# A Flamingo-like block, batches chained: the next batch's scan starts among the finished batch's attention products

## The reference, cut to what matters

```python
# batch 4, length 512, width 512; context width 256; 16 states; feed-forward 2048
x = x + tanh(g_xattn[0]) * mamba(ctx, layernorm(x))          # conv, dt, scan over 512 steps, gate
x = x + tanh(g_ffn[0])   * bitlinear_ffn(layernorm(x))       # ternary weights, 8-bit rows
x = x + tanh(g_xattn[1]) * (layernorm(x) @ softmax(q @ k.T)) # q, k from ctx alone
x = x + tanh(g_ffn[1])   * (gelu(layernorm(x) @ p1.T + b1) @ p2.T + b2)

def mamba(ctx, z):
    x = silu(conv(ctx @ in_proj.T) + conv_b)                  # 512 channels
    dt_low, Bm, Cm = split(x @ x_proj.T)
    dt = softplus(dt_low @ dt_proj.T + dt_b)
    # per channel and state n: h[t] = h[t-1] * exp(dt[t] * A[n]) + dt[t] * x[t] * Bm[n, t]
    # y[t] = sum over n of h[t] * Cm[n, t]
    return (y + D * x) * silu(z)
```

## Time and profile before

| | us |
|---|---|
| median of 3 runs (lowest, highest) | 975.09 (974.25, 976.95) |
| profiled execution | 976.27 |
| its span, first to last instruction | 974.2 |
| TensorE busy | 824.5 (85%) |
| VectorE busy | 776.4 (80%) |
| ScalarE busy | 660.9 (68%) |
| GpSimd busy | 520.0 (53%) |

### The profile page before, as it was taken

One profiled execution on the slowest core, in us unless ns is written; L12 is line 12 of the kernel. 1 busy time (PEld: TensorE's weight loads), 2 busy tenths in 40 slices (PEclk: granted clock), 3 DMA queues, 4 the chain that ended last, 5 costly groups with the idle time before them and its releaser, 6 DMA issues. The chain is left out here.

```text
span 974.2 us, 9381 instructions
## 1 busy us (share of the span) xinstructions
PE 824.5 (85%) x2810; PEld 405.8 (42%) x2810; DVE 776.4 (80%) x905; ACT 660.9 (68%) x984; POOL 520.0 (53%) x461
## 2 busy tenths in 40 slices
PE   6721246799799999999799999998999998898999
PEld 2210012344344344454344444443443444456887
DVE  4589997895889998986899998977889997863333
ACT  4599979573699973774699863773799863624442
POOL 0598785211899883203999881215998871012000
PEclk9755558899899999999899999999899999999999
DMA  8079985001199967301499964301699972201231
GB/s 298 11 142 205 269 202 100 1 1 44 30 201 234 235 145 192 108 2 43 86 212 231 242 140 127 109 1 43 123 225 212 218 164 74 109 1 44 87 108 65
DMA packets 47969, 123.74 MB, mean 127 GB/s; under 512 B 5920, under 2 KB 7072, under 8 KB 47408
## 3 DMA queue, kind: packets, MB, share of 16 engines
q0 software_dynamic: 17280, 62.92, 34.3%
q1 hardware_dynamic: 30640, 60.24, 18.2%
HBM read 56.03 MB, written 4.19 MB: 62 GB/s over the span
## 5 line engine op out<-in xcount | busy, mean ns | idle before, releaser
L1668 POOL TENSOR_TENSOR work<-du,bcast 128x1024 f32<-128x1024 f32 x128 | 352.4, 2780 | 33.8 <-ACT bcast L867 33.2
L1271 DVE TENSOR_TENSOR_SCAN pair<-pair,work 128x512 f32<-128x512 f32 x256 | 299.3, 1215 | 34.4 <-ACT pair L882 28.9
L882 ACT ACTIVATE pair<-dt,a_neg 128x512 f32<-128x512 f32 x256 | 165.8, 682 | 20.2 <-DVE work L1278 17.2
L653 PE MATMUL bank<-stage,ring 128*128 128x512 f32 x384 | 172.9, 593 | 1.5 <-ACT stage L1116 1.5
L1278 DVE TENSOR_TENSOR work<-pair,ccast 128x1024 f32<-128x1024 f32 x128 | 156.8, 1225 | 11.6
L1679 POOL DMA_DIRECT2D u<-work x120 | 130.8, 1090 | 49.0 <-DVE work L1278 20.5
L438 PE MATMUL bank<-xd,pick 128*128 128x512 bf16 x128 | 56.3, 440 | 88.1 <-ACT bcast L867 61.8
L653 PEld LDWEIGHTS bank<-stage,ring 128*128 128x128 f32 x384 | 71.8, 190 | 80.5 <-issue 70.9
L1654 POOL TENSOR_SCALAR fst<-fst 128x1 f32<-128x1 f32 x32 | 9.2, 288 | 166.7 <-DVE fst L1505 166.5
L667 PE MATMUL bank<-ring,stage 128*128 128x512 f32 x192 | 85.6, 594 | 1.7 <-ACT hx L1151 1.7
L438 PEld LDWEIGHTS bank<-xd,pick 128*128 128x128 bf16 x128 | 13.1, 102 | 140.6 <-ACT bcast L867 90.1
(11 more groups left out here) (168 smaller groups left out, 1519.9 us busy)
## 6 DMA issues: line engine op xcount, KB each, us to landing
u<-work POOLq DMA_DIRECT2D x120, 512.0 KB, 6.0
ring<-ffn_dram SPq DMA_DIRECT2D x120, 256.0 KB, 5.0
ring<-ffn_dram SPq DMA_DIRECT2D x16, 512.0 KB, 3.3
xres<-x_dram SPq DMA_DIRECT2D x4, 1024.0 KB, 5.4
stage<-w_dram SPq DMA_DIRECT2D x1, 4096.0 KB, 16.9
stage<-w_dram SPq DMA_DIRECT2D x4, 1024.0 KB, 7.4
out_dram<-stage SPq DMA_DIRECT2D x16, 256.0 KB, 2.1
ctxT<-ctxT_dram SPq DMA_DIRECT2D x4, 512.0 KB, 6.8
```

The source lines that it names most:

```text
L653: last = pe.matmul(banks[2 + f % 2][:], piece(b, f)[:, k * P:(k + 1) * P], xnT[:, k, :], start=k == 0, stop=k == J - 1)
L882: act.activation(pairs[s % DECAYBUFS][:, q, :], dt[:, p * HALF + q, :], ACT.Exp, scale=a_neg[:, p * HALF + q, n:n + 1]).then_inc(s_decay, 1)
L1271: dve.tensor_tensor_scan(pair[:, q, :], pair[:, q, :], rows[:, q, :], 0.0, ALU.mult, ALU.add).then_inc(s_scan, 1)
L1668: pool.tensor_tensor(work[:, s % SCANBUFS, :, :], du[:, p * HALF:(p + 1) * HALF, :], bcast[:, n % 2, :].unsqueeze(1).broadcast_to([P, HALF ...
```

## The change

`attend` writes to banks 1 and 2 in turn and `norm_transpose` only to bank 3, so the scan's pairs no longer wait for `third`. Instead `attend` 2 and 3 wait for `third` 0 and 1, and the first query product for `third` 2. `third` 1, 2, 3 and `norm_apply` 4 to 7 move behind single halves of slots 4 and 5 on VectorE, with their transposes, copies and norms. The up products begin at place 2 of slot 5 instead of 0 and end at place 1 of slot 9; two down pairs more stand in the turning, behind the first three gate transposes. The product of the last but one state (n = 14) is added to `u` by a GpSimd instruction instead of a DMA, with a semaphore of its own, which `last_sum` waits for.

The diff, with the declaration of the semaphore and those hunks left out that only follow it (the copies' bank on ScalarE, and steps that leave an old place):

```diff
@@ -59
 W_LATE = (("scale", 1, 2), ("sign", 1, 2), ("scale", 1, 3), ("sign", 1, 3))
-ATT_BANKS = (4, 6, 7, 6)
+ATT_BANKS = (1, 2, 1, 2)
 MEAN_BANK = 2
...
-FFN_UP = {(5 + f // 4, f % 4): f for f in range(FT)}
-FFN_DOWN = {(9, 0): (0, 0), (9, 1): (0, 2), (9, 2): (0, 4), (10, 0): (0, 6), (10, 1): (0, 8), (10, 2): (0, 10), (10, 3): (0, 12), (11, 0): (0, 14), (11, 2): (1, 0), (11, 3): (1, 2), (12, 0): (1, 4), (12, 1): (1, 6), (12, 2): (1, 8), (12, 3): (1, 10)}
-FOURTH_SLOTS = {(11, 0): 0}
+FFN_UP = {(5 + (f + 2) // 4, (f + 2) % 4): f for f in range(FT)}
+FFN_DOWN = {(9, 2): (0, 0), (9, 3): (0, 2), (10, 0): (0, 4), (10, 1): (0, 6), (10, 2): (0, 8), (10, 3): (0, 10), (11, 0): (0, 12), (11, 1): (0, 14), (11, 2): (1, 0), (11, 3): (1, 2), (12, 0): (1, 4), (12, 1): (1, 6)}
+FOURTH_SLOTS = {(11, 1): 0}
...
@@ -488
             pe.wait_ge(s_qk, b * 2 + 1)
+        elif prev is not None:
+            pe.wait_ge(s_x3, prev * T + 3)
         for k in range(KC):
@@ -567
         gate_transposes(m, (2,))
+        f_pair(b, 1, 8)
+        f_pair(b, 1, 10)
         f_pair(b, 1, 12)
@@ -609
-        bank = 3 if i < T else 2 + i % 2
         if i < T:
             pe.wait_ge(s_x2, b * T + i + 1)
+            pe.wait_ge(s_ev1, b * T + min(i + 2, T))
         else:
             pe.wait_ge(s_xn, b * T + i - T + 1)
-        if i < T:
-            pe.wait_ge(s_ev1, b * T + min(i + 2, T))
-        if i == T - 1:
-            pe.wait_ge(s_xnTc, b * 2 * T + T - 1)
-        if i == T:
-            pe.wait_ge(s_ev0, b * T + T)
-        if i > T:
-            pe.wait_ge(s_xnTc, b * 2 * T + i - 1)
+        if i:
+            pe.wait_ge(s_xnTc, b * 2 * T + i)
         for k in range(J):
             rows = xb[:, i, :] if i < T else xn[:, i % 2, :]
-            last = pe.transpose(banks[bank][:, k * P:(k + 1) * P], rows[:, k * P:(k + 1) * P], ident[:])
+            last = pe.transpose(banks[3][:, k * P:(k + 1) * P], rows[:, k * P:(k + 1) * P], ident[:])
         last.then_inc(s_xnT, 1)
...
         pe.wait_ge(s_xnTc, b * 2 * T + t + 1)
-        if t == 1 and m is not None:
-            pe.wait_ge(s_dt, m * J + J)
         if t == 0:
-            pe.wait_ge(s_gelu, b * T * FC + T * FC)
             pe.wait_ge(s_att, b * J + J)
-        if t == T - 2:
-            pe.wait_ge(s_x2, b * T + T)
-        if t == T - 1:
-            pe.wait_ge(s_x3, b * T + 2)
+            if m is not None:
+                pe.wait_ge(s_dt, m * J + 2)
+        elif t == 1:
+            pe.wait_ge(s_ev0, b * T + T)
+        else:
+            pe.wait_ge(s_x3, b * T + t - 1)
         for k in range(J):
@@ -753
         down1(b, 3)
-        attend(b, 0)
         norm_transpose(b, 2)
-        attend(b, 1, m)
+        attend(b, 0, m)
         scan_bcast(m, 0, 0)
+        norm_transpose(b, 3)
+        attend(b, 1)
+        scan_bcast(m, 1, 0)
         attend(b, 2)
-        scan_bcast(m, 1, 0)
-        norm_transpose(b, 3)
-        norm_transpose(b, 4)
         scan_bcast(m, 0, 1)
         attend(b, 3)
-        norm_transpose(b, 5)
@@ -808
                 qk_products(m, prev, 0)
+            if rest and slot == 5:
+                norm_transpose(b, 5)
             if rest:
@@ -817
                 if rest:
-                    norm_transpose(b, 6)
-                    norm_transpose(b, 7)
+                    norm_transpose(b, 4)
+            if rest and slot == 5:
+                norm_transpose(b, 6)
             if rest:
...
             attention(m, slot, 1, 0)
+            if rest and slot == 5:
+                norm_transpose(b, 7)
             if rest:
@@ -888
                 act.wait_ge(s_dt, b * J + J)
-                if prev is not None:
-                    act.wait_ge(s_x3, prev * T + 1)
                 decay_half(b, 0)
             if n == 0 and part == 0 and prev is not None:
-                act.wait_ge(s_x3, prev * T + T)
+                act.wait_ge(s_x2, prev * T + T)
             if 2 * n + 1 + part < HN:
...
@@ -1174
                 weights(slot)
+            if rest and slot == 5:
+                norm_copy(b, 5)
             if slot != 4:
@@ -1182
                 if rest:
-                    norm_copy(b, 6)
-                    norm_copy(b, 7)
+                    norm_copy(b, 4)
+            if rest and slot == 5:
+                norm_copy(b, 6)
             if rest:
...
             attention(m, prev, slot, 1, 0)
+            if rest and slot == 5:
+                norm_copy(b, 7)
             decays(m, prev, slot, 1, 1)
@@ -1357
         step_inputs(m, 1)
-        norm_apply(b, 4)
-        third(b, 1)
-        norm_apply(b, 5)
-        third(b, 2)
-        third(b, 3)
@@ -1409
         dve.wait_ge(s_hc, (b * HN + HN - 1 + p) * HALF)
-        dve.wait_ge(s_acc[p], (b + 1) * (NS - 1) * 16)
+        dve.wait_ge(s_sum, b * HALF + p + 1)
         dve.tensor_tensor(u[:, js, :], u[:, js, :], work[:, (HN - HALF + p) % SCANBUFS, :, :],
@@ -1591
             if rest and slot == 4:
+                third(b, 1)
+                norm_apply(b, 4)
+            if rest and slot == 5:
+                third(b, 3)
                 norm_apply(b, 6)
+            half(m, prev, slot, 0, 1)
+            if rest and slot == 4:
+                third(b, 2)
+                norm_apply(b, 5)
+            if rest and slot == 5:
                 norm_apply(b, 7)
-            half(m, prev, slot, 0, 1)
             if rest and (slot, 0) in FOURTH_SLOTS:
...
             half(m, prev, slot, 1, 0)
+            if rest and (slot, 1) in FOURTH_SLOTS:
+                fourth(b, FOURTH_SLOTS[slot, 1])
             half(m, prev, slot, 1, 1)
@@ -1616
             state_input(b, prev, p)
-            if prev is not None:
-                norm(prev, T + 2 + p)
+            if prev is not None and p == 0:
+                norm(prev, T)
         for j in range(J):
...
                                ALU.mult, ALU.mult).then_inc(s_accin, 1)
+        if prev is not None:
+            norm(prev, T + 1)
         for s in range(2, AHEAD):
...
@@ -1664
             m, q = divmod(s - SCANBUFS, 2)
-            pool.wait_ge(s_acc[q], (b * (NS - 1) + m + 1) * 16)
+            pool.wait_ge(s_acc[q], (b * (NS - 2) + m + 1) * 16)
         pool.tensor_tensor(work[:, s % SCANBUFS, :, :], du[:, p * HALF:(p + 1) * HALF, :],
@@ -1674
         if n:
-            pool.wait_ge(s_acc[p], (b * (NS - 1) + n) * 16)
+            pool.wait_ge(s_acc[p], (b * (NS - 2) + n) * 16)
         carry_wait(pool, "pool")
-        pool.dma_start(u[:, p * HALF:(p + 1) * HALF, :], work[:, s % SCANBUFS, :, :],
-                       accum_op=ALU.add).then_inc(s_acc[p], 16)
+        js = slice(p * HALF, (p + 1) * HALF)
+        if n == NS - 2:
+            pool.tensor_tensor(u[:, js, :], u[:, js, :], work[:, s % SCANBUFS, :, :], ALU.add).then_inc(s_sum, 1)
+        else:
+            pool.dma_start(u[:, js, :], work[:, s % SCANBUFS, :, :], accum_op=ALU.add).then_inc(s_acc[p], 16)
@@ -1770
         for slot in range(4, SLOTS):
-            if rest and slot == 5:
-                bias(b, 2)
             half(m, prev, slot, 0, 0)
             if rest and slot == 4:
+                norm(b, 6)
+            if rest and slot == 5:
                 bias(b, 0)
-            if rest and slot == 5:
-                bias(b, 3)
+            if rest and slot == 6:
+                bias(b, 2)
             if not rest:
...
             if rest and slot == 4:
+                norm(b, 7)
+            if rest and slot == 5:
                 bias(b, 1)
+            if rest and slot == 6:
+                bias(b, 3)
             half(m, prev, slot, 1, 0)
...
```

More of the change, by code:

```diff
@@ L267, in program @@
         s_acc = [sem(f"s_acc{p}") for p in range(HALF)]
+        s_sum = sem("s_sum")
         s_last = sem("s_last")
@@ L1007, in between @@
                 first_copy(m, b, 0, 1)
-                norm_copy(b, 4)
             def closing(b):
@@ L1111, in norm_copy @@
                     act.wait_ge(s_xm, b * T + t + 1)
-                bank = 3 if i < T else 2 + i % 2
                 if parts:
                     act.activation(in_parts(x_high[:, :, t * P:(t + 1) * P]),
-                                   banks[bank][:].rearrange("p (k l) -> p k l", k=J), ACT.Copy)
-                act.activation(xnT[:, :, t * P:(t + 1) * P], banks[bank][:].rearrange("p (k l) -> p k l", k=J),
+                                   banks[3][:].rearrange("p (k l) -> p k l", k=J), ACT.Copy)
+                act.activation(xnT[:, :, t * P:(t + 1) * P], banks[3][:].rearrange("p (k l) -> p k l", k=J),
                                ACT.Copy).then_inc(s_xnTc, 1)
@@ L1167, in pass_ @@
                         decays(m, prev, slot, 0, 1)
-                        if rest:
-                            norm_copy(b, 5)
                     copy_next(m, slot, 0, 0)
@@ L1636, in between @@
                 norm(b, 3)
-                norm(b, 4)
-                norm(b, 5)
                 start_sum(m, b)
```

## The result

The changed kernel takes 1025.8 us (median of 4 runs, 1024.05 to 1026.5) against 975.05 (974.25 to 976.95) of the kernel before on the same chip: ratio 1.0506, 95% interval 1.0485 to 1.0527. The forecast was 998 us, 982 to 1007. The direction was right; the loss is 50.7 us where 22.6 were summed up. The profiled execution has a span of 1024.5 us (before 974.2).

What follows compares the result with a forecast made beforehand. TensorE, busy 197.75 of a pass's 212.1 us, was taken as the bound, VectorE second. Three passes x 8.1, first scan -2.1 and closing +0.4 gave +22.6 us, so 998 us, range 982 to 1007.

Steps and rivals of the forecast that it cites:

- Part 1: Start of the scan in a pass: it begins 3.4 us earlier, at 459.65.
- Part 2: Start of the up products: 8.8 us later, at 484.1, with 1.2 us taken for stalls of four applies.
- Part 6: Behind the gates: q's transpose moves 8.1 us later per pass, closing +0.4; DMAs, bias additions and moved norms cost nothing.
- Part 3: TensorE's clock at the start of the up products: half rate costs 1.5 us, bounds 0 and 2.6.
- Part 4: Up and down products: first up to first down stays 62.2 us; then two pairs save 6.87, fewer waits 2.2.
- Part 5: Last partial sum: its 3.2 us DMA wait goes, off the path in passes; the first scan gains 2.1 us.
- (c): Rival, worse: applies stall 4.7 us, clock costs 2.6, few waits won back; 1008 us; 0.15 including no earlier scan.
- (b): Rival, faster: work fills TensorE's 5.45 us hole, up products start no later than 475.27; 970 us; chance 0.07.

Runs made afterwards that it cites:

- e7: Changed kernel with norm_apply also writing out a sum nobody reads, a form that doesn't take the shared port: 1005.53 us, ratio 1.0306.
- e8: e6 with the four applies per pass on ScalarE, and the third half's decays and one GpSimd norm moved: 959.18 us, ratio 0.9825.
- e10: e8 with the change's feed-forward tables: up products two places later, matching down products, two pairs behind the gates: 978.92 us, ratio 1.0031.
- e6: Changed kernel rebuilt: thirds 1, 2 and applies 4, 5 ahead of the scan, feed-forward tables of before, bias additions late: 989.12 us, ratio 1.0137.
- e1: Kernel before with one part of the change alone, state 14's product added to u by GpSimd instead of a DMA: 973.55 us, ratio 0.9972.
- e11: e9 with ScalarE's applies 4 and 5 one place earlier and half 3's decays behind the next broadcast copies: median 968.59 us, ratio 0.9927.
- e2: Changed kernel with the four GpSimd bias additions two slots later, nothing else: 1012.69 us, ratio 1.0366.
- e9: e1 plus the four applies per pass on ScalarE, scan still behind all four attention products: 981.96 us, ratio 1.0063.
- e4: Changed kernel with 24 idle bf16 matmuls on TensorE ahead of the last norm transpose: 1023.06 us, ratio 1.0474.

## Why the prediction was wrong in size

**Part 1, the scan's start: right** within 0.2 us. **Part 2: the step that failed**, in its term for the stalls of the applies. "I take 0.3 (nearest to the median), 1.2 in all", bounds 0 to 2 each. Measured in the three passes: the fourth apply 6.40, 6.39 and 6.38, another one 2.06, 1.60 and 3.25. What the four take beyond 0.52 each is 7.4, 7.0 and 8.6 us a pass for the 1.2 taken: 19.4 us too little in three passes. Up to the start of the last apply the forecast held: it comes 37.1 us behind the end of `down1` (460.50 to 497.62), for 36.7 by its terms (445.04 to 481.7). From there to the first up product 2.4 us were forecast, and it took 8.25. e7, where no apply stalls, has the 38.6 that the terms give. Of the 27.6 us that the sum missed, this row of the table has 19.7. Of the sixteen applies in the earlier trace rows three met one product of GpSimd (2.57 each) and the others gaps or short instructions. The change sets the last one behind a product, with a bias addition, a DMA issue, a second product and a second bias addition ready behind it. GpSimd, kernel after:

```profile
495.44 2.64 POOL L1673 TENSOR_TENSOR work<-du,bcast 128x1024 f32<-128x1024 f32 x1
497.75 1.55 POOL L1739 TENSOR_TENSOR stage<-stage,b 128x512 f32<-128x512 f32 x1
498.96 1.18 POOL L1688 DMA_DIRECT2D u<-work  x1
499.56 2.95 POOL L1673 TENSOR_TENSOR work<-du,bcast 128x1024 f32<-128x1024 f32 x1
501.87 1.86 POOL L1739 TENSOR_TENSOR stage<-stage,b 128x512 f32<-128x512 f32 x1
508.93 0.90 POOL L1688 DMA_DIRECT2D u<-work  x1 [5.21 <-issue]
```

The apply, begun at 497.62, ends at 504.01, 0.3 us behind the end of this run of five instructions (503.73). A bound of 2 us, less than one product, was the mistake: here the apply waited until GpSimd's run ended. The third apply shows the same from the other side: it ends at 494.12, 0.3 behind the end of one product (493.83), after which GpSimd stood still for 0.09 us only. "Bias additions ... move on GpSimd, which has room: nothing" (Part 6) was wrong for the same reason: it has room, but their place closed the gap in which VectorE would have got in.

That GpSimd has no idle time isn't enough by itself. In the kernel before, the two applies at 466.65 took 0.78 and 0.91 while GpSimd's instructions stood back to back:

```profile
465.12 2.86 POOL L1623 TENSOR_SCALAR u<-u,pch 128x512 f32<-128x512 f32 x4
467.95 4.81 POOL L1668 TENSOR_TENSOR work<-du,bcast 128x1024 f32<-128x1024 f32 x2
```

In that run each record begins within 0.03 us of the end of the one before; in the runs that held VectorE for 5.65 to 6.40 each begins 0.3 to 0.6 us ahead of it (by spans that are rough). What decides whether VectorE is let in between two instructions stays open: no run varies it.

The Trainium skill (SBUF — State Buffer, "Who interferes with whom") says that whoever starts first holds the shared pair for its whole instruction, and that the form of `tensor_scalar` that also writes out its accumulator doesn't use it. The second agrees with e7 (0.77 to 0.81 us, always). By the first the wait would have been at most one product, 2.95 us; 6.39 says that VectorE wasn't let in between these instructions of GpSimd. The measurement decides.

**Part 3, the clock: right in kind.** Three stretches, ahead of the last wait, at the start of the up products and 5 us on (columns as in the earlier trace rows):

```profile
496.00:497.00 1.00, 0.61 (x1) 0.11 (x1) 0.90 (x2) 0.68 (x2) 1.00 (x1) 0.50 0.91 176
506.00:508.00 2.00, 2.00 (x3) 0.97 (x4) 1.91 (x3) 0.38 (x1) 0.00 (x0) 0.50 0.00 0
511.00:513.00 2.00, 2.00 (x6) 0.95 (x5) 2.00 (x3) 1.32 (x2) 2.00 (x3) 1.00 1.13 197
```

The clock is at 1.2 GHz already at 496, before the wait of 7.22 begins (496.86), and at 2.4 GHz again by 511. The stalled apply isn't its cause: in e7, whose longest wait there is 1.57, it is 0.50 as well (488.3 to 498.5). The first eight matmuls take 5.54 for 3.70: 1.8 us for the 1.5 taken. The Trainium skill (TensorE: Matmul & The Clock Gate, "Part 4: PE-mode transpose") says that transposes don't count as activity. No run shows transposes alone: among short transposes and broadcasts with waits under 1.7 us the clock fell in e7 and stayed at 1.00 in e8.

**Part 4, up to down: "62.2 us as before" was wrong by 3.9.** 1.8 is the clock, 1.2 the longer wait of the first down group for ScalarE, 0.9 two energy products that moved in from the next stretch. "Moving their places by one state keeps their order against the rest" isn't so: e10 has 3.5 of it without any stalled apply, 1.4 of them the clock again. **Down to gates:** -7.9, -8.1, -8.0 for -9.1. 6.9 are the two pairs and 0.9 the energy products that left this stretch, so in sum next to nothing was won back, for 2.2 taken. TensorE's idle time fell by 0.7 only (3.35 to 2.64), and the clock took some 2 us: the group of sixteen down products at 607.89, behind a wait of 2.10 for `fourth`, which the change puts one place later, takes 9.05 us where 7.03 is the full rate. A last -1.6 isn't split here.

**Part 5: right.** The last sums don't wait, the first gates come 3.0 earlier (2.1), the rest is off the path. **Part 6: right**, 6.8 per turning for 6.87; the closing gained 1.0 instead of losing 0.4.

**The rivals and the range.** (c) named the cause, stalls beside GpSimd, and still priced them at half a product each. Its sum is wrong as well: 8.1 and its own 3.5, 1.1 and 1.2 make 13.9 a pass and 1015, not 11.5 and 1008. The upper end of the range, 10.5 a pass, leaves out the forecast's own bound of 2 us for each apply: with it and the other upper bounds the terms make 17.2 a pass, 1025. That this is the measured time is luck, since a single apply went beyond its bound by far. (b) said what a faster version needs: up products before 30.2 behind the end of `down1`, and work in the hole. e8 is such a version (26.0), with the feed-forward tables of before. e6, the same idea with the applies on VectorE, lost 14 us.

So of the change's parts: GpSimd's addition gains 3 us (e1), the early scan is worth between 2 (e8 against e11's faster executions) and 9 (by the medians), the half slot costs about 20 (e10 against e8, the clock's part in it), and the stalled applies about 20 (e7 against the change), 13 of which are the bias additions' place (e2). These were measured in different surroundings and needn't add up.

## What to carry to other kernels

Before moving a VectorE instruction of a two-port form into a stretch where GpSimd is busy, list what GpSimd has ready behind it: in these runs the stall lasted up to the end of a whole run of GpSimd instructions, at the least to the end of one product, and a median from a stretch with other neighbours says nothing on it. If such an instruction stands on the path of the bounding engine, give it to ScalarE, and then read ScalarE's order again, since a copy queued behind a waiting decay costs as much as the stall did (e9). Starting one engine's stage earlier gains only what the bounding engine gets earlier: the scan came some 3 us sooner in both the 1026 and the 959 us kernel. And read the clock in every stretch before crediting a difference of 2 or 3 us to a schedule: in e1, e8 and e11 a fall of the clock moved that much from one stretch to another.

## What was not expected of the hardware

- A 0.52 us `tensor_scalar` took 6.38 to 6.40 us in all three passes, in pass 1 over the end of one product of GpSimd, two bias additions, a DMA issue and a second product. In e6 the same happened with products and DMA issues alone (5.65 or 5.66 for one).
- VectorE's scans and products by C, which read one input from PSUM and one from SBUF, kept their 1.20 to 1.23 us beside GpSimd's work, the product at 496.48 beside that same run too. An instruction with both large inputs in SBUF didn't: `u<-xpad,pch,u` took 2.46 for its usual 0.75 once in each pass of the changed kernel (at 424.13 in pass 1), begun during a GpSimd instruction of 2.76 us.
- ScalarE does the same apply in 0.80 to 0.82 us whatever GpSimd does, 0.3 more than the undisturbed 0.52 of VectorE.
- 24 idle matmuls kept the clock up in the pass where they ended 0.7 us ahead of the next work, and not where they ended 2.2 or 3.2 us ahead (e4).
- The clock fell to 0.50 in a stretch without a wait (e8, 434.8). In the kernel before it did so at the same place in passes 0 and 2 (0.50 at 228 and at 655) and not in pass 1, though the instructions are the same.
